# Context attention of two stages: weighing by three bf16 products of split terms, masks of the rest on 128 rows, GpSimd's work laid between the steps

## The reference, cut to what is touched

```
scores = einsum('bhqd,bhkd->bhqk', q / sqrt(DH), k)
scores = where(mask[:, None], -1e18, scores)          # stage 4 alone
attn = softmax(scores, axis=-1)
context = einsum('bhqk,bhkd->bhqd', attn, v)
return context.transpose(0, 2, 1, 3).reshape(b, -1, H * DH) @ Wo.T + bo
```

## Time and profile before

| | us |
|---|---|
| median of three runs (1933.63 to 1936.42) | 1933.74 |
| the profiled execution's own time | 1927.72 |
| its span | 1925.9 |
| stage 4's units, from the first score to the last exp | about 1096 to 1262 |
| stage 6's units | about 1496 to 1596 |

### The profile page before, as it was taken

The page is one execution under the profiler, slowest core; times in us unless marked ns, Lnnn a source line. Parts: engine busy times, 40 slices in busy tenths (PEclk is TensorE's granted clock), DMA queues, the critical chain, the costliest instruction groups (busy, mean ns, idle before and its releaser), DMA issues.

```text
span 1925.9 us, 31970 instructions
## 1 busy us (share of the span) xinstructions
PE 1497.9 (78%) x11459; PEld 982.9 (51%) x11581; DVE 1175.3 (61%) x2856; ACT 802.1 (42%) x1803; POOL 754.6 (39%) x906
## 2 busy tenths in 40 slices
PE   4899979979998977574278789958976885568877
PEld 2677757766776765452255345524443333324444
DVE  4777677767767655538847657644565555644443
ACT  3677657747765644320034245533212542201111
POOL 3688678857756863500012343000002101233330
PEclk9999999999999997776568799989986987778887
DMA  6233211211211112400000000000000000000000
GB/s 241 63 102 106 74 55 42 55 36 38 54 41 45 52 33 72 161 5 1 0 1 1 11 4 1 1 1 1 1 1 1 1 1 1 1 0 6 1 6 11
DMA packets 35442, 63.93 MB, mean 33 GB/s; under 512 B 7527, under 2 KB 25026, under 8 KB 34131
## 3 DMA queue, kind: packets, MB, share of 16 engines
q1 hardware_dynamic: 33815, 59.77, 10.4%
q0 software_dynamic: 1472, 2.12, 0.4%
HBM read 30.59 MB, written 12.66 MB: 22 GB/s over the span
## 4 chain that ended last, share of the span: by engine, by line
PE 63%; DVE 23%; issue 4%; POOL 4%; ACT 4%; DMA 1%; SPq 0%; DVEq 0%; ACTq 0%; POOLq 0%
PE banks L475 15%; PE banks L694 8%; PE banks L709 6%; PE banks L683 6%; PE banks L1876 3%; DVE xn L421 3%; PE banks L1859 2%; PE banks L450 2%; DVE work L744 2%; PE banks L2546 2%; DVE norm_room L405 1%; PE banks L2497 1%; PE banks L1785 1%; PE banks L1826 1%; POOL work L963 1%
## 5 line engine op out<-in xcount | busy, mean ns | idle before, releaser
L963 POOL TENSOR_TENSOR work<-work 128x512 bf16<-128x512 f32 (+1 forms) x448 | 372.6, 861 | 48.3 <-ACT work L852 45.0
L837 ACT ACTIVATE work<-banks,work 128x666 f32<-128x666 f32 x256 | 209.2, 817 | 200.6 <-DVE work L744 165.7
L415 POOL TENSOR_TENSOR norm_room<-norm_room,minus_half 128x4 f32<-128x4 f32 x48 | 50.1, 1044 | 542.3 <-DVE norm_room L410 542.3
L744 DVE TENSOR_REDUCE work<-banks 128x1 f32<-128x666 f32 x256 | 216.3, 845 | 61.2 <-PE banks L683 60.8
L694 PE MATMUL banks<-const,work 128*128 128x128 f32 (+1 forms) x1536 | 218.0, 279 | 31.2 <-ACT work L852 26.1
L694 PEld LDWEIGHTS banks<-const,work 128*128 128x128 f32 (+1 forms) x1536 | 155.9, 135 | 53.0 <-ACT work L837 29.4
L758 DVE COPY work<-banks 128x256 f32<-128x256 f32 x256 | 106.9, 418 | 122.2 <-PE banks L694 122.1
L683 PE MATMUL banks<-work 128*128 128x154 bf16 (+1 forms) x932 | 170.6, 302 | 11.5 <-DMA work<-work 6.4
L475 PE MATMUL banks<-work,weights_b 128*128 128x512 bf16 (+1 forms) x830 | 157.4, 347 | 13.3 <-DVE work L2200 5.6
L709 PE MATMUL banks<-work 128*64 128x256 bf16 x2304 | 158.6, 282 | 8.3 <-POOL work L963 7.1
L852 ACT ACTIVATE work<-banks 128x512 f32<-128x512 f32 x256 | 151.2, 591 | 9.5 <-PE banks L694 9.4
(11 more groups left out here) (390 smaller groups left out, 3006.8 us busy)
## 6 DMA issues: line engine op xcount, KB each, us to landing
work<-work SPq DMA_DIRECT2D x128, 166.5 KB, 3.0
sorted<-in_pads SPq DMA_DIRECT2D x10, 838.5 KB
weights_b<-in_weights SPq DMA_DIRECT2D x1, 4120.0 KB, 23.9
work<-scratch SPq DMA_DIRECT2D x64, 64.0 KB, 2.0
weights_b<-in_weights SPq DMA_DIRECT2D x1, 2824.0 KB, 9.8
weights_a<-in_weights SPq DMA_DIRECT2D x1, 2056.0 KB, 8.5
weights_a<-in_weights SPq DMA_DIRECT2D x1, 2050.0 KB, 10.1
work<-work SPq DMA_DIRECT2D x32, 64.0 KB, 1.9
```

Of the source, the lines that this page charges most:

```text
L744: ve.tensor_reduce(self.neg_max[i % 4], self.slot[i % 2][:, 0:KEYS0], AX_X, ALU.max, negate=True).then_inc(self.mark("max"))
L837: ac.activation(self.probs[i % 3], self.slot[i % 2][:, 0:KEYS0], ACT.Exp, bias=self.neg_max[i % 4], accum_out=self.sums[u % 4][:, 2 * j + ...
L963: po.tensor_tensor(parts[:, :, :, 0], exact, parts[:, :, :, 1], ALU.subtract).then_inc(self.mark(event, i - 3))
```

## The change

What it does:

- **weigh**: each exp term and each value stays where it is as an fp32 word, and is read as two bf16 halves: the upper half of the word, and a lower half that a subtraction (whole minus upper half) writes into the word's lower two bytes. A weigh is then three groups of four products with values (high with high, high with low, low with high) and two groups with ones, 20 bf16 matmuls of 256 columns instead of 8 fp32 ones.
- **the subtractions** ("low"): one per term. In stage 4 those of g = 0 are DVE's, the other three of a chunk GpSimd's; in stage 6 all are GpSimd's. GpSimd also makes those of the values, two instructions a batch. A weigh waits for them (`term_low`, `term_low_0`, `values_low`).
- **places**: weigh(c) comes after the terms of chunk c + 2 instead of c + 1, the last one at u + 2.33; divide and finish move back a little; TERMS is 16 instead of 12.
- **the mask of the rest**: the product has 128 rows instead of 26. The tile is cleared once for it (two memsets).
- **GpSimd's order**: it now follows `context_items` too; a batch's heads are five separate items.

The core of the diff:

```diff
--- before.py
+++ after.py
@@ -57,7 +57,7 @@
 
 
 GROUPS, WIDE = 4, P // 4
-HALF, TERMS = SEQ // 2, 12
+HALF, TERMS = SEQ // 2, 16
 
 
 WEIGHTS = [
@@ -187,7 +187,7 @@
 
 ONCE = {"similarity": "router_steps", "router_gate": "router_steps", "square": "router_steps", "squares": "router_steps",
         "bq_scaled": "filled", "bv_wide": "filled", "clear_shift": "filled", "context_rest": "filled", "ones": "filled",
-        "clear": "filled", "tokens": "filled", "wo_low": "filled", "mixed_low": "low_b", "summed": "router_steps", "ranked": "routed",
+        "clear": "filled", "tokens": "filled", "wo_low": "filled", "mixed_low": "low_b", "term_low": "low_b", "values_low": "low_b", "term_low_0": "placed", "summed": "router_steps", "ranked": "routed",
         "places": "placed", "clean": "router_steps", "padded": "router_steps", "relative": "router_steps", "delta": "router_steps",
         "mix": "router_steps", "gates": "gate_steps", "gate_exp": "gate_steps"}
 
@@ -1751,12 +1751,17 @@
             terms = []
             for c in range(a.chunks):
                 terms += [("term", u, c, g) for g in range(GROUPS)]
-                if c:
-                    terms.append(("weigh", u, c - 1, 0))
-            terms.append(("weigh", u, a.chunks - 1, 0))
+                if c >= 2:
+                    terms.append(("weigh", u, c - 2, 0))
+            terms.append(("weigh", u, a.chunks - 2, 0))
             out += [(u + 1.38 + 0.88 * i / len(terms), *item) for i, item in enumerate(terms)]
-            out += [(u + 2.27 + 0.1 * j, "divide", u, j, 0) for j in range(2)]
-            out.append((u + 2.56, "finish", u, 0, 0))
+            out += [(u + 1.44 + 0.88 * i / len(terms), "low", *item[1:]) for i, item in enumerate(terms) if item[0] == "term"]
+            out.append((u + 2.33, "weigh", u, a.chunks - 1, 0))
+            out += [(u + 2.36 + 0.1 * j, "divide", u, j, 0) for j in range(2)]
+            out.append((u + 2.6, "finish", u, 0, 0))
+        for b in range(1, BATCH):
+            out += [(2 * b - 1.6, "mask", b, 0, 0), (2 * b - 0.8, "query_low", b, 0, 0), (2 * b + 0.3, "mask_t", b, 0, 0)]
+            out += [(2 * b - 1.5 + 0.12 * g, "heads", b, g, 0) for g in range(GROUPS + 1)]
         if a.stage == 4:
             out += [(1.2, "measure", 3, BATCH - 1, 0), (1.6, "scale", 3, BATCH - 1, 0), (2.2, "turn", 3, BATCH - 1, 0)]
             for b in range(BATCH - 1):
@@ -1858,23 +1863,27 @@
                 left = a.keys[b % 3][:, h + c, 0:P] if c < a.per_group else a.keys_rest[b % 3][:, h:h + c, :].rearrange("p h k -> p (h k)")
                 m = pe.matmul(bank, left, a.q4[b % 2][:, g, cols], start=True, stop=s != 4)
                 if s == 4:
-                    mask = a.mask_t[b % 2]
-                    if c < a.per_group:
-                        m = pe.matmul(bank, self.cb["eye_b"], mask[:, 0, cols], start=False, stop=True)
-                    else:
-                        m = pe.matmul(bank, self.cb["four_eyes"][0:CTX_REST, :], mask[0:CTX_REST, 1, cols], start=False, stop=True)
+                    mask, rest = a.mask_t[b % 2], c == a.per_group
+                    m = pe.matmul(bank, self.cb["four_eyes" if rest else "eye_b"], mask[:, int(rest), cols], start=False, stop=True)
                 m.then_inc(self.mark("termed", s, n))
             elif what == "weigh":
                 if c == 0:
                     self.bank(pe, 5, "divided", s, u, 1)
-                    pe.wait_ge(*self.at("values", s, b))
+                    pe.wait_ge(*self.at("values_low", s, b))
                 n, rows_n, _, _ = self.term(a, u, c, GROUPS - 1)
-                pe.wait_ge(*self.at("exp4", s, n))
-                for of_sums in (0, 1):
+                pe.wait_ge(*self.at("term_low", s, n))
+                if s == 4:
+                    pe.wait_ge(*self.at("term_low_0", s, n - GROUPS + 1))
+                terms = [self.halves(self.term(a, u, c, g)[3]) for g in range(GROUPS)]
+                values = [self.halves(a.values[b % 2][0:rows_n, c, g, :]) for g in range(GROUPS)]
+                for of_values, of_terms in ((1, 1), (1, 0), (0, 1)):
                     for g in range(GROUPS):
-                        left = a.block[0:rows_n, c, :] if of_sums else a.values[b % 2][0:rows_n, c, g, :]
-                        m = pe.matmul(self.bank_of(5)[WIDE * g:WIDE * (g + 1), of_sums * HALF:(of_sums + 1) * HALF], left,
-                                      self.term(a, u, c, g)[3], start=c == 0 and not of_sums, stop=c == a.chunks - 1, skip_group_check=True)
+                        pe.matmul(self.bank_of(5)[WIDE * g:WIDE * (g + 1), 0:HALF], values[g][:, :, of_values], terms[g][:, :, of_terms],
+                                  start=c == 0 and of_values == of_terms == 1, stop=False, skip_group_check=True)
+                for of_terms in (1, 0):
+                    for g in range(GROUPS):
+                        m = pe.matmul(self.bank_of(5)[WIDE * g:WIDE * (g + 1), HALF:SEQ], self.halves(a.block[0:rows_n, c, :])[:, :, 1],
+                                      terms[g][:, :, of_terms], start=False, stop=c == a.chunks - 1, skip_group_check=True)
                 m.then_inc(self.mark("weighed", s, u, c))
             elif what == "finish":
                 bank = self.bank(pe, 7, *brought(u))
@@ -1968,6 +1977,11 @@
                 ve.wait_ge(*(self.at("lifted", s, u - 2) if u >= 2 else self.at("clear_shift", s)))
                 ve.wait_ge(*self.own("ve", ve.tensor_copy(out[:, :, 0, :], most)))
                 ve.tensor_tensor(out[:, :, 1, :], most, out[:, :, 0, :], ALU.subtract).then_inc(self.mark("shift", s, u))
+            elif what == "low" and s == 4 and g == 0:
+                n, _, _, whole = self.term(a, u, c, g)
+                ve.wait_ge(*self.at("exp4", s, n))
+                ve.tensor_tensor(self.halves(whole)[:, :, 0], whole, self.halves(whole)[:, :, 1],
+                                 ALU.subtract).then_inc(self.mark("term_low_0", s, n))
             elif what == "divide":
                 at = slice(c * P, (c + 1) * P)
                 ve.wait_ge(*self.at("weighed", s, u, a.chunks - 1))
@@ -1983,18 +1997,18 @@
             elif what == "scale":
                 self.follow_scale(ve, u, c)
 
-    def heads_of(self, po, a, b):
-
-        last = 2 * a.chunks * GROUPS
-        if b >= 3:
-            po.wait_ge(*self.at("termed", a.stage, (b - 2) * last - 1))
-        for g in range(GROUPS):
+    def heads_of(self, po, a, b, g):
+
+        if b >= 3 and g == 0:
+            po.wait_ge(*self.at("termed", a.stage, (b - 2) * 2 * a.chunks * GROUPS - 1))
+        if g < GROUPS:
             if b in (0, 2):
                 po.wait_ge(*self.at(("key_rows_a", "key_rows_b")[b // 2], a.stage, g))
             heads = slice(g * a.per_group, (g + 1) * a.per_group)
             wide = [P, a.per_group, CTX]
             po.tensor_tensor(a.keys[b % 3][:, heads, :], a.k4[:, g, b * CTX:(b + 1) * CTX].unsqueeze(1).to_broadcast(wide),
                              a.head_of[:, heads].unsqueeze(2).to_broadcast(wide), ALU.mult).then_inc(self.mark("key_heads", a.stage, b, g))
+            return
         rest = [P, GROUPS, a.per_group, CTX_REST]
         po.tensor_tensor(a.keys_rest[b % 3].rearrange("p (g h) k -> p g h k", g=GROUPS),
                          a.k4[:, :, b * CTX + P:(b + 1) * CTX].unsqueeze(2).to_broadcast(rest),
@@ -2012,26 +2026,40 @@
         if s == 4:
             self.mask_po(po, 0)
         self.query_low(po, a, 0)
-        self.heads_of(po, a, 0)
+        for g in range(GROUPS + 1):
+            self.heads_of(po, a, 0, g)
         for n in (0, 1):
             i = po.memset(a.shift[n][:, :, :, :], 0.0)
         i.then_inc(self.mark("clear_shift", s))
         po.tensor_copy(a.context_rest.rearrange("p b (h k) -> p b h k", h=a.per_group),
                        self.context[:, :, P:CTX].unsqueeze(2).to_broadcast([P, BATCH, a.per_group, CTX_REST])).then_inc(self.mark("context_rest", s))
         if s == 4:
+            for mask in a.mask_t:
+                i = po.memset(mask[:, 1, :], 0.0)
+            po.wait_ge(*self.own("po", i))
             self.mask_t_po(po, a, 0)
-            self.follow_power(po, 3, BATCH - 1)
-        for b in range(1, BATCH):
-            if s == 4:
-                self.mask_po(po, b)
-            self.heads_of(po, a, b)
-            self.query_low(po, a, b)
-            if s == 4:
-                if b >= 2:
-                    self.follow_power(po, 4, b - 2)
-                self.mask_t_po(po, a, b)
-        if s == 4:
-            self.follow_power(po, 4, BATCH - 2)
+        for what, u, c, g in self.context_items(a):
+            if what == "low" and (s != 4 or g):
+                n, _, _, whole = self.term(a, u, c, g)
+                po.wait_ge(*self.at("exp4", s, n))
+                po.tensor_tensor(self.halves(whole)[:, :, 0], whole, self.halves(whole)[:, :, 1],
+                                 ALU.subtract).then_inc(self.mark("term_low", s, n))
```

(16 more changed lines are left out.)

## The result

The changed kernel takes 1959.88 us (median of 4 runs, 1952.13 to 1964.51); the kernel before took 1933.68 us beside it. The ratio is 1.0121, 95% interval 1.0093 to 1.0148: slower by 1.2%, where 1923.0 us and a range from 1910 to 1938 had been forecast. A second series of both gave 1.0154 (1.0117 to 1.0191).

The account below looks back on a forecast made before the run. PE sets stage 4's pace; chains between engines take part of stage 6. Stage 4 -10.6, stage 6 -1.7, clock +1.5: -10.8 from the profiled 1927.7 gives 1916.9, or 1923.0 us with the median's 6 us offset; range 1910 to 1938.

Parts of the forecast that it names:

- mask on 128 rows: Stage 4, the rest's mask: 0.22 us saved 32 times between term, mask and next product, -7.0 us.
- start, GpSimd's order: Start of stage 4: GpSimd makes batch 1's mask, heads and query_low before the power, shortening PE's wait, -5.8 us.
- shorter weighing: PE's weigh falls from 1.00 to 0.73 us: -10.8 us in stage 4, -4.9 in stage 6.
- subtractions: Lows on GpSimd and DVE: +13.0 us in stage 4; in stage 6 +2.2 and +1 at the end.
- VectorE's +4.5: Stage 4, DVE's five lows a unit at 0.75 us: 0.9 us in each of five units, bounds 0 and +11.
- DVE goes on when GpSimd's instruction ends: A DVE instruction beside GpSimd waits for one GpSimd instruction, so a low on DVE costs 0.45 to 1.02 us.
- rival 1: DVE becomes stage 4's pace, each low costing 1.02 us instead of 0.75: about +9, 1932 us, chance 0.18.
- GpSimd's queue: Stage 4: lows behind heads, values and query_low delay weigh(3) in two units, +2.8 and +4.7 us; stage 6, +2.2.
- Rival 2: GpSimd's lows take 0.75 us instead of 0.57, PE's clock falling behind waits: +15, 1938 us, chance 0.14.
- The moved divide and finish ... cost nothing: Moved divide and finish, larger ring of terms and values_low cost nothing as long as the other terms hold.
- clock +1.5: Stage 6: PE waits more often; one more unit at 0.71 of the clock would cost 3.7 us, +1.5 taken.
- Its own signs of being wrong: Wrong if DVE's waits hold PE, a weigh takes 1 us or more, or stage 4's clock falls below 0.95.

Follow-up runs that it names:

- e5_mask: The kernel before with only the mask of the rest changed to 128 rows, its bank cleared by GpSimd: ratio 0.9965.
- e16_oldall: The changed kernel with fp32 weighing, no subtractions and the old order of steps in stages 4 and 6; 128-row mask and GpSimd's new order kept: ratio 0.9927.
- e9_fp32: The changed kernel with the fp32 weighing of before and no subtractions; mask, GpSimd's new order and new steps kept: ratio 1.0022.
- e3_nolow: The changed kernel without any subtraction, upper halves used twice with as many matmuls, low halves left out of the result: 1915.81 us, ratio 0.9866.
- e6_gap: The changed kernel with GpSimd waiting for its own last instruction before most subtractions and each head and query_low: 1964.94 us, ratio 1.0136.
- e4_allpo: The changed kernel with VectorE's five subtractions a unit in stage 4 moved to GpSimd too: 1960.02 us, ratio 1.0093.
- e14_old6: The changed kernel with fp32 weighing, no subtractions and the old order of steps in stage 6 alone: ratio 0.9950.
- e8_both: The changed kernel with a batch's heads spread over two units and GpSimd waiting for its own last instruction: 1964.46 us, ratio 1.0125.
- e13_evengap: The changed kernel with a batch's heads in the even units and GpSimd waiting for its own last instruction: 1949.84 us, ratio 1.0093.
- e15_all4: The changed kernel with even-unit heads and GpSimd gaps, bf16 weighing in stage 4 only, stage 6 weighing and steps as before: 1932.53 us, ratio 1.0001.

## Why the prediction was wrong

Differences of the table take stage 4 apart, one step after another; other orders of the steps were not run, so parts may shift between neighbours:

| stage 4 | predicted | measured | from |
|---|---|---|---|
| mask on 128 rows | -7.0 | -6.7 | before (second profile) to e5_mask |
| start, GpSimd's order (and 16 term buffers) | -5.8 | -8.2 | e5_mask to e16_oldall |
| new order of steps | 0 | +3.2 | e16_oldall to e9_fp32 |
| shorter weighing | -10.8 | -9.0 | e9_fp32 to e3_nolow |
| subtractions | +13.0 | +31.8 | e3_nolow to changed |

The term that failed most is the last: +13.0 for the subtractions of stage 4, which cost 31.8. By units, with e3_nolow beside the changed kernel, 18.8 of them lie in units 1 and 3 (+7.5 forecast) and 9.7 in units 5 to 7, where 1 us and the share of VectorE's +4.5 stood. Two steps of the prediction are wrong behind it, what a VectorE instruction waits for and how full GpSimd is; how the 31.8 us divide between the two no run shows. The other failed term is the one put at nothing, the moved steps.

- **Weighing and mask: right.** The first rows are a rest term and its mask, 0.11 apart; then a weigh from 1133.77 to the next line at 1134.47, 0.70 us where 0.73 was forecast and the earlier trace rows has 1.00:

```profile
1132.24 0.27 PE L1864 MATMUL banks<-work 128*104 128x256 bf16 x1
1132.35 0.27 PE L1867 MATMUL banks<-work,const_b 128*104 128x256 bf16 x1
1132.46 0.27 PE L1864 MATMUL banks<-work 128*104 128x256 bf16 x1
...
1133.77 0.54 PE L1881 MATMUL banks<-work 128*32 128x256 bf16 x12
1134.13 0.41 PE L1885 MATMUL banks<-work,const 128*32 128x256 bf16 x8
1134.47 0.66 PE L450 MATMUL banks<-const,xn 128*128 128x128 f32 x4
```

- **The start: right, and too small by 2.4 us.** The start went from 40.4 to 32.2 us, with the old steps and the old weighing.
- **"DVE goes on when GpSimd's instruction ends": the step that failed.** It was read off L1970 at 1.15 us and four scalings of one head each, places where GpSimd's row was short or VectorE's instruction was let in. It holds for all but one of VectorE's forty subtractions, 0.4 to 1.2 us (mean of the 128-row ones 0.71, forecast 0.75; the one took 3.90), but not in a backlog of GpSimd, where a copy of 0.18 us stood for 7.62. A price for each of the forty subtractions was worked out, and none for the 0.2 us instructions around them (rival 1 names negate without a price), which carried 16.8 us for eight copies:

```profile
L1983 DVE TENSOR_TENSOR work<-work 128x256 bf16<-128x256 f32 x32 | 22.7, 710 | 1.7 <-ACT work L1941 1.7
L1978 DVE CAST work<-work 128x32 bf16<-128x32 f32 x8 | 16.8, 2105 | 0.3
```

- **GpSimd's queue: right mechanism, too small.** The odd unit's sum was 16.5 us. In the profile those 23 instructions take 17.3, and the mask of the next batch (1.75) and the end of mask_t (0.5), which the sum left out for unit 1, bring it to the 19.6 measured. mask_t stands ahead of both rows (it ends at 1138.52 and 1183.75), so units 1 and 3 are alike, not the second heavier. The sum also has a slip: 0.95 of 15.4 us is 14.6, not 14.8, which makes +3.0 of its +2.8. That PE would wait for the subtractions in them was the forecast; the waits appeared under VectorE's name, since its stall came first, and e6_gap and e4_allpo showed GpSimd's own: 17 to 20 us, against +2.8 and +4.7 forecast. With the stall gone the odd unit was still 24.5 us in both, where 18.2 and 20.1 had been worked out.
- **Rival 1 named the engine, at 1932 us.** It had each subtraction blocked for one instruction. The Trainium skill (SBUF — State Buffer, Who interferes with whom), cited there, says that the loser is blocked for the other's whole instruction; the trace shows a copy blocked through eleven in a row, 7.62 us, and the measurement decides. **Rival 2's** price of a GpSimd instruction did not come true (0.646 us each in units 0 to 2, overlapped by 0.04), but the fall of the clock behind PE's waits did: for 5 us after the wait at 1157.67 it was 0.50.
- **"The moved divide and finish ... cost nothing": wrong.** With the weighs, which moved with them, they cost 3.2 us in stage 4 and 11 to 12.5 in stage 6 (kernel before and e14_old6 to e9_fp32), of which a draw may be a part: with the old steps and fp32 weighing six profiles lie between 118.9 and 125.4, with the new ones both at 131.4. From there the shorter weighing gave 7.7 us back (e3_nolow 123.7; -4.9 forecast) and the subtractions took 11 to 13 (137.1 and 134.9; +3.2 forecast). The term "clock +1.5" was all that stood for a clock lost there.
- **Its own signs of being wrong.** Two of the three came: VectorE's waits held PE, and the granted clock of stage 4 fell to 0.91 (0.97 before), 0.87 and 0.86 in units 1 and 3. GpSimd was busy for 80% of units 1 and 3, where over 90% had been expected.
- **The two first profiles lie further apart than the medians.** The kernel before was profiled 6 us under its median and the changed one 4.6 us over its own. Of the 36.8 us between their spans, 28.2 lie in stages 4 and 6 and 7.5 ahead of stage 4's first score, in unchanged code. The medians differ by 26.2. The prediction had allowed for its 6 us.

## What to carry to other kernels

Before work is given to an idle engine, look for the smallest instructions of its neighbour that the critical engine waits for, and price them for a whole unbroken row of the new work, not for one instruction of it; two engines that look half idle over a stage can both be full in one unit. When removing a stall leaves the time as it was, look which wait has taken its place: here the two kernels that freed VectorE's copy and took nothing off GpSimd stayed at 1.0093 and 1.0136 of the kernel before, and only with room on GpSimd did the same cure shorten the unit (22.2 to 18.9 us). Moving a step "a little later" is not free: give it a term. Try to keep independent matmuls between two results that come from another engine one after the other.

## What the runs showed of the hardware

- A VectorE instruction between SBUF and SBUF can stand beside a row of overlapping GpSimd instructions through many of them: 7.62, 7.63, 7.31 and 6.01 us here, and 3.85 beside subtractions alone. Instructions that read the matmul banks in the same stretches kept their time (L1962, 0.47 us). Gaps of 0.08 us, made by a wait of GpSimd on itself, let it in within 1.5 us (e6_gap, e8_both, e13_evengap, e15_all4). Why most of VectorE's subtractions got in after one or two instructions of such rows, and why the stalled ones came through where they did, is not settled.
- PE's clock fell behind waits of at most 1.02 us each: behind 0.52 and 1.02 us it ran at 1.2 GHz for 6.7 us, behind 0.46, 1.02 and 0.52 for 13.6, and the unit of those 92 matmuls took 5.7 us more than e14_old6's at 2.4 GHz. The same waits can come without it: e14_old6's first even unit kept 2.4 GHz, its second lost 10.2 us of it.
- A four-tile bf16 weigh of 20 matmuls with 256 columns each takes 0.70 us.
- Twenty profiles with the same code ahead of stage 4 reached its first score up to 16 us apart, and two profiles of one program differed by 5 us in stage 6.
